# Decoder kernel, one core: latent matrix products formed in the Fourier stage's first group, one block for the joined last stage

## The reference, cut to what matters

```
# latent cross-attention, per head h (dim_head 64, D = 128)
scores_h = (latents Wq_h) (X Wk_h)^T / 8      = latents (Wq_h Wk_h^T / 8) X^T   -> A_h = Wq_h Wk_h^T / 8
out     += softmax(scores_h) X Wv_h Wout_h    = softmax(scores_h) X (Wv_h Wout_h) -> N_h = Wv_h Wout_h
# bit-linear feed-forward
weight_quant(w) = clip(round(w / mean|w|), -1, 1) * mean|w|      (w1: 512x128, w2: 128x512)
# layer norm before each of them: (x - mean) / sqrt(var + 1e-5)
```

## Time and profile before

| | us |
|---|---|
| timed runs | 1704.3, 1704.57, 1708.15 (median 1704.57) |
| the profiled execution, its own time | 1708.87 |
| its span | 1707.1 |
| mean granted clock of the PE | 0.943 of full |

### The profile page before, as it was taken

How to read it: one execution, slowest core, us unless ns; L and a number is a source line. 1 busy time by engine, 2 the same in 40 slices (tenths; PEclk the granted TensorE clock), 3 DMA queues, 4 the chain that set the end, 5 groups by cost and what they waited for, 6 DMA issues and landing times. The chain is left out here.

```text
span 1707.1 us, 31412 instructions
## 1 busy us (share of the span) xinstructions
PE 1466.3 (86%) x12306; PEld 897.9 (53%) x12306; DVE 1104.4 (65%) x2343; ACT 916.9 (54%) x1255; POOL 310.2 (18%) x285
## 2 busy tenths in 40 slices
PE   5999869999897888788887836999999999999973
PEld 3666547776564334343333334566666666666542
DVE  3676556665332888889888821445576767676777
ACT  1323224433454788898888923445555565665433
POOL 3333234442001111110110002112111211210001
PEclk9999979999899899999999966999999999999985
DMA  4000000000000000000000010222222222222220
GB/s 158 2 2 2 2 22 11 15 8 2 1 1 1 1 1 1 1 1 1 1 1 1 1 59 7 59 72 53 66 68 57 64 70 62 56 67 63 57 53 16
DMA packets 39825, 50.73 MB, mean 30 GB/s; under 512 B 9216, under 2 KB 21632, under 8 KB 39296
## 3 DMA queue, kind: packets, MB, share of 16 engines
q1 hardware_dynamic: 39392, 48.06, 10.6%
q10 hardware_dynamic: 288, 0.67, 0.1%
HBM read 13.04 MB, written 2.10 MB: 9 GB/s over the span
## 5 line engine op out<-in xcount | busy, mean ns | idle before, releaser
L1542 DVE TENSOR_TENSOR l_px<-psum,l_share 128x1024 f32<-128x1024 f32 x64 | 78.4, 1225 | 158.9 <-PE psum L1275 98.0
L1407 ACT ACTIVATE l_prob<-psum,l_bias 128x1024 f32<-128x1024 f32 x64 | 71.4, 1115 | 174.8 <-PE psum L1255 174.8
L1264 PE MATMUL psum<-l_XT,l_A 128*128 128x256 f32 x512 | 132.4, 404 | 8.7 <-ACT l_th L1415 6.0
L1250 PE MATMUL psum<-l_th,l_XT 128*128 128x512 f32 x256 | 125.5, 613 | 1.0 <-DVE stream L1549 0.5
L1308 PE MATMUL psum<-l_px,l_N 128*128 128x256 f32 x512 | 124.8, 387 | 1.6 <-ACT l_r L1445 1.6
L1275 PE MATMUL psum<-l_prob,l_X 128*128 128x512 f32 x256 | 123.1, 604 | 0.0
L1264 PEld LDWEIGHTS psum<-l_XT,l_A 128*128 128x128 f32 x512 | 96.9, 200 | 23.0 <-ACT l_th L1415 8.1
L1523 DVE TENSOR_REDUCE l_top<-psum 128x8 bf16<-128x1024 f32 x64 | 78.1, 1221 | 42.9 <-PE psum L1323 42.9
L1308 PEld LDWEIGHTS psum<-l_px,l_N 128*128 128x128 f32 x512 | 94.6, 192 | 18.9 <-issue 4.7
L786 PE MATMUL psum<-f_projX,f_kT 64*128 64x512 f32 x256 | 74.1, 657 | 34.7 <-DVE f_frac L1013 19.2
L788 PE MATMUL psum<-f_qT,f_projX 64*128 64x512 f32 x256 | 73.1, 647 | 32.5 <-DVE f_frac L1013 23.9
(11 more groups left out here) (283 smaller groups left out, 3279.7 us busy)
## 6 DMA issues: line engine op xcount, KB each, us to landing
l_share<-l_recip SPq DMA_DIRECT2D x512, 64.0 KB, 2.0
early_weights<-in_weights SPq DMA_DIRECT2D x1, 2405.0 KB, 15.8
c_cs<-in_ctx SPq DMA_DIRECT2D x16, 128.0 KB, 2.1
l_mats<-in_l_mats SPq DMA_DIRECT2D x1, 2048.0 KB, 7.5
l_craw<-in_ctx SPq DMA_DIRECT2D x16, 128.0 KB, 2.3
out<-l_normed SPq DMA_DIRECT2D x16, 128.0 KB, 2.0
late_weights<-in_weights SPq DMA_DIRECT2D x1, 1089.0 KB, 11.0
relbias<-in_relbias ACTq DMA_DIRECT2D x1, 512.0 KB, 4.9
```

Source lines behind the costliest of these rows:

```text
L1250: nc.tensor.matmul(ps[:, SC + n, :], XT[:, q % 3, k, :, :], th[:, q % 2, k, 8 * n:8 * n + 8, :], start=True, stop=False)
L1264: last = nc.tensor.matmul(ps[:, RO + j // 2, (j % 2) * 256:(j % 2 + 1) * 256], A[:, QB * k + j, :], XT[:, q % 3, :, 1, :], start=True, sto ...
L1407: nc.scalar.activation(prob[:, b % 4, :, :], ps[:, SC:SC + 2, :], ACT.Exp, bias=bias[:, b:b + 1]).then_inc(s["exped"], 1)
L1542: nc.vector.tensor_tensor(px[:, q % 2, :, k, :], ps[:, GA:GA + 2, :].rearrange("p a (h s) -> p (a h) s", s=S), share[:, (b // 2) % 2, b % ...
```

## The change

- `l_A` and `l_N` are kept for the whole program (allocated in `build`).
- The 2 MB load of `mats` is issued by SP at the start of the Fourier stage, into the half of `qf` that the first queries use later.
- The PE makes the products in four rounds of 8 heads in Fourier units N = 1 to 4 of the first group (`latent_products`), in banks 6 and 7, behind `key_values(N-1)`; each round after the first waits for ACT's copies of the round before it. ACT copies a round in the same unit (`keep_products`, two copies), behind `features(N)`, and waits for the round to be made.
- The first block of the joined stage is gone. Its reciprocal deviations and masks open the one block that is left; the weights are measured at step -7, their magnitudes summed by PE at step -6 and the weights quantised by DVE at step -3, in tile `r`. The mask's load stands between the two first context loads.
- New waits: `masked` (ACT's first exponent, POOL's first preparation), `wsteps` (first combine, hidden, activate), `ab_sb` (first turned key-values), `ab_ps` (features of unit 8).

```diff
@@ fourier_phase
+    mats = qf[:, 0, :, :, :].rearrange("p a b c -> p (a b c)").rearrange("p (m j d) -> p m j d", m=4, d=P)
+        @block.sync
+        def _(sp):
+            sp.dma_start(mats, c["l_mats"]).then_inc(s["mats_in"], 16)
+            def latent_products(r):
+                if r == 0:
+                    pe.wait_ge(s["mats_in"], 16)
+                    pe.wait_ge(s["v_sb"], 1)
+                    pe.wait_ge(s["q_sb"], 1)
+                else:
+                    pe.wait_ge(s["ab_sb"], 2 * r)
+                of = r // 2 * 2
+                for h in range(8 * (r % 2), 8 * (r % 2) + 8):
+                    par = h % 2
+                    rows = slice(par * S, par * S + S)
+                    at = (h % 8 // 2) * P
+                    last = nc.tensor.matmul(ps[:, 6 + par, at:at + P], mats[rows, of, h // 2, :], mats[rows, of + 1, h // 2, :],
+                                            start=True, stop=True)
+                last.then_inc(s["ab_ps"], 1)
             def turn_key_values(g, pair):
+                if g == 0 and pair == 0:
+                    pe.wait_ge(s["ab_sb"], 8)
@@ PE loop
                     if 1 <= n <= KEYS:
                         key_values(N - 1)
+                    if 1 <= N <= 4:
+                        latent_products(N - 1)
@@ ACT
+            def keep_products(r):
+                act.wait_ge(s["ab_ps"], r + 1)
+                for par in range(2):
+                    heads = slice(8 * (r % 2) + par, 8 * (r % 2) + 8, 2)
+                    out = (c["l_A"] if r < 2 else c["l_N"])[:, heads, :]
+                    nc.scalar.activation(out, ps[:, 6 + par, :].rearrange("p (h d) -> p h d", d=P), ACT.Copy,
+                                         scale=0.125 if r < 2 else 1.0).then_inc(s["ab_sb"], 1)
@@ ACT loop
                 if g < G:
+                    if N == KEYS:
+                        act.wait_ge(s["ab_ps"], 4)
                     features(N)
+                    if 1 <= N <= 4:
+                        keep_products(N - 1)
@@ latents_bitlinear_phase
-    with ExitStack() as early:
...
-                sp.dma_start(mats[:, :, :, :], c["l_mats"]).then_inc(s["mats_in"], 16)
-                sp.dma_start(mask[:, :], c["mask"]).then_inc(s["mask_in"], 16)
...
             context_in(0)
+            sp.dma_start(mask[:, :], c["mask"]).then_inc(s["mask_in"], 16)
             context_in(1)
@@ PE loop
             for i in range(FIRST, LAST):
+                if i == -6:
+                    pe.wait_ge(s["mags"], 1)
+                    nc.tensor.matmul(ps[:, YB, 0:2], ones32[:, :], mags[:, :], start=True, stop=True).then_inc(s["mag_ps"], 1)
@@ ACT, ahead of its loop
+            act.wait_ge(s["stats2"], 1)
+            nc.scalar.activation(rstd2[:, :], rstd2[:, :], ACT.Sqrt)
+            nc.scalar.activation(rstdc[:, :], rstdc[:, :], ACT.Sqrt).then_inc(s["root2"], 1)
@@ DVE
+            scales_begun()
+            masks()
+            scales_ended()
             for i in range(FIRST, LAST):
+                if i == -7:
+                    weights_measured()
+                if i == -3:
+                    weights_quantised()
```

More of the change, by code:

```diff
@@ L709, in fourier_phase @@
         "consts lifted staged based xT_ps xT_sb k_ps k_sb v_ps v_sb q_ps q_sb z_ps reduced rounded wrapped feats kv_ps kv_sb kvT_ps kvT_sb o_ps o_sb "
-        "y_ps yT_sb yt_ps steps out_read").split()}
+        "y_ps yT_sb yt_ps steps out_read mats_in ab_ps ab_sb").split()}
     w, ps = c["w"], c["psum"]
@@ L1068, in latents_bitlinear_phase @@
     s = {n: c["sem"](f"{name}_{n}") for n in (
-        "mats_in mask_in ab_ps ab_sb stats2 root2 prep mags mag_ps wsteps quant "
+        "mask_in masked stats2 root2 prep mags mag_ps wsteps quant "
         "ctx_in0 ctx_in1 scaled prep0 prep1 prep2 staged latT_ps XT_sb XT16 X_ps X_sb th_ps th_sb rough top scores exped sums sums_read recip share00 share01 share10 share11 "
@@ L1085, in latents_bitlinear_phase @@
     keep, drop, bias = sb("keep", [P, NT]), sb("drop", [P, NT]), sb("bias", [P, B])
-    A, N = sb("A", [P, H, P]), sb("N", [P, H, P])
+    A, N = c["l_A"], c["l_N"]
+    mask = sb("mask", [P, NT + B], mybir.dt.uint8)
+    mags, wscale = sb("mags", [P, 2]), sb("wscale", [P, 2])
     ones32 = sb("ones32", [P, P])
@@ L1089, in latents_bitlinear_phase @@
     raw = [w("b_w1"), w("b_w2")]
-    with ExitStack() as early:
[L1092 to L1098, removed]
-                sp.dma_start(mats[:, :, :, :], c["l_mats"]).then_inc(s["mats_in"], 16)
-                sp.dma_start(mask[:, :], c["mask"]).then_inc(s["mask_in"], 16)
[L1102 to L1159, removed]
-                dve.wait_ge(s["root2"], 1)
-                nc.vector.reciprocal(rstd2[:, :], rstd2[:, :]).then_inc(s["prep"], 1)
-                nc.vector.reciprocal(rstdc[:, :], rstdc[:, :])
-                dve.wait_ge(s["prep"], 3)
-                nc.vector.tensor_tensor(rstd2[:, :], rstd2[:, :], rstd[:, :], ALU.mult)
@@ L1302, in combine @@
             def combine(q, k):
+                if q == 0 and k == 0:
+                    pe.wait_ge(s["wsteps"], 1)
                 if k == 0:
@@ L1334, in hidden @@
                 pe.wait_ge(s["xiT_sb"], q + 1)
+                if q == 0:
+                    pe.wait_ge(s["wsteps"], 5)
                 for t in range(TQ):
@@ L1403, in exponent @@
                 act.wait_ge(s["scores"], b + 1)
+                if b == 0:
+                    act.wait_ge(s["masked"], 2)
                 if b >= 4:
@@ L1440, in activate @@
                 act.wait_ge(s["deq1"], q + 1)
+                if q == 0:
+                    act.wait_ge(s["wsteps"], 5)
                 if q >= 1:
@@ new lines, in masks, with scales_ended @@
+            def masks():
+                dve.wait_ge(s["mask_in"], 16)
+                nc.vector.tensor_scalar(keep[:, :], mask[:, 0:NT], 1.0, None, ALU.mult)
+                nc.vector.tensor_scalar(drop[:, :], mask[:, 0:NT], -1.0, 1.0, ALU.mult, ALU.add).then_inc(s["masked"], 1)
+                nc.vector.tensor_scalar(bias[:, :], mask[:, NT:NT + B], 1e30, 1e30, ALU.mult, ALU.subtract).then_inc(s["masked"], 1)
+            def scales_ended():
+                dve.wait_ge(s["root2"], 1)
+                nc.vector.reciprocal(rstd2[:, :], rstd2[:, :]).then_inc(s["prep"], 1)
+                nc.vector.reciprocal(rstdc[:, :], rstdc[:, :]).then_inc(s["prep"], 1)
+                dve.wait_ge(s["prep"], 3)
+                nc.vector.tensor_tensor(rstd2[:, :], rstd2[:, :], rstd[:, :], ALU.mult).then_inc(s["prep"], 1)
+                dve.wait_ge(s["prep"], 5)
@@ new lines, in weights_measured, with weights_quantised @@
+            def weights_measured():
+                nc.vector.memset(ones32[:, :], 1.0)
+                nc.vector.memset(eps[:, :], EPS_NORM)
+                for n in range(2):
+                    last = nc.vector.tensor_reduce(mags[:, n:n + 1], raw[n], AX.X, ALU.add, apply_absolute_value=True)
+                last.then_inc(s["mags"], 1)
+            def weights_quantised():
+                dve.wait_ge(s["mag_ps"], 1)
+                nc.vector.tensor_scalar(wmean[:, :], ps[:, YB, 0:2], 1.0 / (P * HID), EPS_Q, ALU.mult, ALU.max).then_inc(s["wsteps"], 1)
+                dve.wait_ge(s["wsteps"], 1)
+                nc.vector.reciprocal(wscale[:, :], wmean[:, :]).then_inc(s["wsteps"], 1)
+                dve.wait_ge(s["wsteps"], 2)
+                for n in range(2):
+                    last = nc.vector.tensor_scalar(r[:, n, :], raw[n], wscale[:, n:n + 1], None, ALU.mult)
+                last.then_inc(s["wsteps"], 1)
+                dve.wait_ge(s["wsteps"], 3)
+                nc.vector.tensor_scalar(r[:, :, :], r[:, :, :], MAGIC, MAGIC, ALU.add, ALU.subtract).then_inc(s["wsteps"], 1)
+                dve.wait_ge(s["wsteps"], 4)
+                nc.vector.tensor_scalar(wq[:, :, :], r[:, :, :], -1.0, 1.0, ALU.max, ALU.min).then_inc(s["wsteps"], 1)
@@ L1685, in prepare @@
                 pool.wait_ge(s["prep1"], q + 1)
+                if q == 0:
+                    pool.wait_ge(s["masked"], 1)
                 nc.gpsimd.tensor_tensor(gx[:, 0, :, :], cx[:, :, :], group(keep, q), ALU.mult)
@@ L1760, in build @@
             "psum": ctx.enter_context(nc.psum_tensor("psum", [P, 8, 512], F32)),
+            "l_A": sb("l_A", [P, H, P]), "l_N": sb("l_N", [P, H, P]),
             "l_mats": ins["l_mats"], "mask": ins["mask"],
```

7 lines of the change are left out of this document (added).

## The result

| | before | changed |
|---|---|---|
| timed runs, median (lowest to highest), us | 1705.66 (1704.3 to 1708.15), 4 | 1687.10 (1682.13 to 1688.41), 4 |
| profiled execution, span, us | 1707.1 | 1686.6 |
| mean granted clock of the PE | 0.943 | 0.953 |

The changed kernel takes 0.9884 of the time before (95% interval 0.986 to 0.9908): 18.6 us less. Forecast were 12.8 us less and 1691.8 us, range 1683 to 1700. The sign and the range hold; the size is short by about 6 us, and that is what the experiments had to find.

What follows compares the result with a forecast made beforehand. PE was taken to bound the joined stage's middle, and PE, DVE and ACT together the Fourier stage. Joined stage -19.4 and products +6.6 gave -12.8 us, from median 1704.57 to 1691.8 us; range 1683 to 1700.

Steps and rivals of the forecast that it cites:

- The joined stage: Joined stage's start: without its first block, the first preparation starts 19.4 us sooner, or 14.3 if the mask lands late.
- Rival C: Joined stage's start: the mask's load is slow by itself, 7.3 us; gain only 7.7 us, 1696.9 us; chance 0.06.
- The covers: Joined stage: POOL's work and DVE's idle time hide weight measuring and quantising; otherwise at most 2.1 + 2.9 us worse.
- The first group: Fourier stage, units 1 to 7: ACT's product copies and its 3.9 us wait for round 0 make it 6.6 us late.
- The step that failed: Fourier stage after the first group: ACT and DVE stay equally late, 6.6 us, and the rest moves as one piece.
- part 2: Making the weight products in the Fourier stage costs 6.6 us; floor 2.5 us, ceiling 15 us.
- rival A: Fourier stage: the ring of PE, DVE and ACT absorbs more of the products; gain 17 us, 1687.6 us; chance 0.17.
- The clock: PE's granted clock, priced at the joined stage's start: left at nil, some 10 us possible, usual luck 4 us either way.
- floor of 2.5: Fourier stage's first group: least lateness, if only the copies' 4.4 us count and ACT's 1.9 us idle is used up.
- B: Fourier stage: PE stays at low clock through product rounds 1 to 3; gain only 4.4 us, 1700.2 us; chance 0.10.
- D: Joined stage: without the products before it, PE stays at 0.50 clock longer; slower, 1711.8 us; chance 0.05.

Runs made afterwards that it cites:

- Experiment 6: The changed kernel with each pair of ACT's product copies one unit later, behind features(2) to features(5): ratio 0.9908 to the kernel before.
- experiment 5: The changed kernel with product rounds 0 and 1 ahead of unit 0, rounds 2 and 3 in units 0 and 2: ratio 0.9897 to the kernel before.
- experiment 1: The changed kernel run again unchanged: ratio 0.9906 to the kernel before, median 1689.0 us.
- experiment 8: The changed kernel without products and their 2 MB load, with four ACT copies of 1800 columns as delay: ratio 0.9917 to the kernel before, mean 1692.1 us.
- experiment 4: The kernel before with four useless ACT copies of 2048 columns in Fourier units 1 to 4: ratio 1.0029 to the kernel before, median 1708.4 us.
- experiment 3: The changed kernel with the joined stage's first block kept, products still made in the Fourier stage: ratio 0.9939 to the kernel before, median 1697.1 us.
- experiment 7: The changed kernel with weights measured and quantised ahead of the joined stage's first preparation, still one block: ratio 0.9892 to the kernel before.

## Why the prediction was right, and where it fell short

**The joined stage: right.** Forecast 19.4, measured 19.9 us. DVE starts on the mask 1.77 us after its issue, where 2.16 were taken for the landing, and had waited 1.42 us for it. Rival C is out: without the load ahead of it the mask doesn't take the 7.3 us of the earlier trace rows. The Trainium skill's rule that was read as speaking for it (DMA: Bandwidth & Descriptors, Specifications) is one for the rate of transfers; no run here measures that rate, and the traces show only that rows of 96 bytes don't make this landing slow. The covers held: the magnitudes ran during POOL's work, the quantisation before DVE's next idle 15.78 us ended at 1031.95. From the block's start to the end of the span 21.8 us are gone, where about 19 were to show; 1.9 of them fall behind the first preparation, within what that part varies.

**The first group: right in mechanism, 1 us too much.** ACT's wait for round 0 was forecast at 3.9 and is 3.92 us; features(2) at 574.7 and came at 574.6; lift(7)'s subtraction at 589.3 and came at 588.4, in part because a pair of copies takes 1.0 us from start to start (575.53 to 576.50) and not 1.1. The second group's preparation by POOL came 5.6 us late; 6 to 7 were to show. 6.6 us became 5.6. By the same account, with 3.9 for the four pairs: 3.9 + 3.9 of waiting - 1.9 of idle time is 5.9. Experiment 6 confirms the wait's share (2.0 us less waiting, 2.0 less in the group); experiment 5 takes 3.0 away, but moves the table load and the PE's clock too.

**The step that failed** is the one behind it: "From there ACT and DVE are equally late, and the rest of the stage moves as one piece." It moved as one piece in its work, not in its clock. A group takes about 1.5 us more for each low stretch that it meets (52.1, 53.8, 55.2, 56.7), and which groups meet one differs between the kernels and between executions of one. Five traces with the products in units 1 to 4 average 387.4 us for the seven pieces, four traces without 394.3: 6.9 us back for 5.6 paid, though one of the five (experiment 1) gave nothing back there. The timed runs need no trace: the changed kernel's 16 runs have a mean of 1687.0 us (standard error 0.7), the 12 without products 1687.9 (1.1). In the whole part 2 costs -0.9 us, give or take 2.8: the 5.6 us are excluded, a cost of up to 2 us is not. The sum is then -19.9 + 0, against 19.1 measured (48 runs of the kernel before, mean 1706.1). So the term of the forecast that was wrong is the +6.6 us of part 2: it was right for the first group and about 0 for the whole. That the result still fell into the range is luck: the range reached down to 1683 for the sake of rival A, which isn't what happened. The clock was left at nil with 4 us of luck "either way"; in four traces of five it was a term with a sign.

**Rivals.** A forecast 1687.6 and is nearest in number, but by another way: the ring didn't absorb the copies, and the first group was 5.6 us late, not near its floor of 2.5. B: rounds 1 to 3 took 1.16 us on PE, not 2.0. D: in this pair the clock at the joined stage's start is the same row for row, at 0.50 until 23.7 us behind the first preparation before and 23.6 in the changed kernel. In the other traces without the products in that gap it rises 12 to 24 us behind the first preparation (12.6 in experiment 1), and in the kernel before once more at 18.0, so taking 8 us of PE work out didn't hold the clock down. The Trainium skill's rule beside it (TensorE: Matmul & The Clock Gate, What's actually happening) is not contradicted: the products before had released nothing.

**What stays open.** Why the seven pieces meet fewer low stretches in four traces of five with the products in units 1 to 4 isn't shown. A delay of ACT alone doesn't bring it in the timed runs: experiment 8 is 4.2 us above the kernel without products in the mean for 4.4 us of delay (standard error of the difference 2.1), experiment 4 is 5.1 us above the kernel before for 6.4. Products placed otherwise don't bring it either: experiments 5 and 6 enter sooner, have nine low stretches each and means of 1688.7 and 1690.8 us. So neither the timing alone nor the PE's work alone was shown to be the cause; a delay of just 5.6 us without products, and a profile of more than one execution of it, are what is missing. That experiment 3 is 8 us slower and only 4.9 in its first preparation was not followed: the mean of its 12 runs is 1695.2 us with a standard error of 1.6, so 3 us of the 8 may be scatter.

## What to carry to other kernels

Work that depends on nothing but weights belongs out of a serial gap between stages: there every microsecond of load, product and copy counts in full (15.0 of the 19.9 us here), while in a busy pipeline it may disappear. When an engine's copy is put behind work of its own unit, count not the copy but the wait for its input: in the first group ACT stood still for 3.9 us, as long as its four pairs of copies took together. And where the lengths of a stage's pieces follow the PE's granted clock, as in this ring, a cost of 5 us in one group need not reach the end, nor a saving of 3: judge such edits by the mean of many runs first. One profile is one execution: here its Fourier stage and its joined stage each varied by 6 to 7 us between executions of one kernel.

## What the runs showed of the hardware that was not expected

- DVE and POOL slow each other in some operations. In the changed kernel the quantisation (L1658 to L1663) runs beside POOL's preparation; timeline:

```profile
1004.08 0.68 DVE L1648 TENSOR_REDUCE l_mags<-late_weights 128x1 f32<-128x512 f32 x1
1004.09 0.72 POOL L1709 TENSOR_TENSOR l_gx<-l_lat,late_weights 128x256 f32<-128x256 f32 x1 [129.27 <-DVE stream L1494]
...
1012.26 1.65 DVE L1658 TENSOR_SCALAR l_r<-late_weights,l_wscale 128x512 f32<-128x512 f32 x2
1012.72 0.91 POOL L1710 TENSOR_TENSOR l_gx<-l_cx,late_weights 128x256 f32<-128x256 f32 x1
...
1013.94 1.10 DVE L1661 TENSOR_SCALAR l_r<-l_r 128x1024 f32<-128x1024 f32 x1
1014.45 1.17 POOL L1713 TENSOR_TENSOR l_cx<-l_gx,late_weights 128x256 f32<-128x256 f32 x1
```

The 1024-column DVE operation takes 1.10 us, and 0.69 where POOL is idle (experiment 7's row at 1000.21); the two 512-column ones 1.65 together against 0.88 in experiment 7. POOL's own take up to 1.17 us in place of 0.72. The reduction at 1004.08 slows nothing: it takes 0.68 us beside POOL's 0.72, and 0.68 without POOL in experiment 7 too. Both engines had the time here.
- What stands ahead of an engine's first operation of a new kind can move a table load: in experiment 5 it came behind the copies, at 564.17, and held the first features back by its 1.28 us; in the changed kernel it ran at 557.59 in ACT's idle time.
- The same kernel's group lengths fall on few values (52.1, 53.8, 55.2, 56.7 us), and the first one or two after the first group repeat between executions to 0.1 us.
